# Two late stages of a twelve-layer network on one core: without TensorE's products of constants in its waits

## What is computed

```python
x = x + _L3_xattn_ref(_layernorm(x), ctx_1024, mask_BxS2_ik0, ...)   # stage 9
x = x + _L3_attn_ref(_layernorm(x), ...)                             # stage 10
x = x + _L3_ffn_ref(_layernorm(x), ...)                              # stage 11
```

## Time and profile before

| | |
|---|---|
| median of 3 runs | 1437.22 us (1436.2 to 1438.24) |
| profiled execution, its own time | 1435.54 us |
| span from first to last instruction | 1433.8 us |
| mean granted TensorE clock | 0.989 of full |
| busy share: PE, VectorE, ScalarE, GpSimd | 96%, 66%, 56%, 26% |
| stage 10, about | 1199.2 to 1253.5 us |
| stage 11, about | 1253.5 us to the end |

### The profile page before, as it was taken

The page is one execution under the profiler, slowest core; times in us unless marked ns, Lnnn a source line. Parts: engine busy times, 40 slices in busy tenths (PEclk is TensorE's granted clock), DMA queues, the critical chain, the costliest instruction groups (busy, mean ns, idle before and its releaser), DMA issues.

```text
span 1433.8 us, 24150 instructions
## 1 busy us (share of the span) xinstructions
PE 1376.1 (96%) x9532; PEld 973.4 (68%) x9541; DVE 953.4 (66%) x1559; ACT 805.6 (56%) x1481; POOL 370.4 (26%) x485
## 2 busy tenths in 40 slices
PE   7999999999999999999999989999999998999897
PEld 4897668886998676998567645555555554645686
DVE  5676744335786576786366578889999973566533
ACT  5774344344665555664555437778888884325232
POOL 3986332002642204542101332222121200100100
PEclk9999999999999999999999989999999999999999
DMA  9413342234214513212316255353535404210140
GB/s 372 156 56 132 129 171 81 89 95 166 97 60 152 194 60 126 97 60 76 130 72 272 76 198 167 121 183 123 194 129 183 152 2 189 89 59 2 59 177 15
DMA packets 49072, 177.77 MB, mean 124 GB/s; under 512 B 4864, under 2 KB 6144, under 8 KB 43008
## 3 DMA queue, kind: packets, MB, share of 16 engines
q1 hardware_dynamic: 48960, 176.23, 34.3%
HBM read 132.66 MB, written 44.60 MB: 124 GB/s over the span
## 4 chain that ended last, share of the span: by engine, by line
PE 74%; DVE 7%; ACT 3%; issue 1%; POOL 0%; ACTq 0%; DVEq 0%
PE PS L160 44%; PE PS L2387 9%; PE PS L2291 7%; PE PS L2305 4%; PE PS L630 2%; DVE SM L2402 2%; PE PS L1877 1%; PE PS L1898 1%; PE PS L2378 1%; PE PS L1905 1%; PE PS L2875 1%; PE PS L266 1%; DVE CNr L3094 0%; PE PS L1635 0%; ACT L283 0%
## 5 line engine op out<-in xcount | busy, mean ns | idle before, releaser
L2402 DVE TENSOR_REDUCE SM<-PS 128x1 f32<-128x1024 f32 x256 | 310.6, 1223 | 34.4 <-PE PS L2291 31.1
L160 PE MATMUL PS<-ARr 128*128 128x256 f32 (+1 forms) x1024 | 269.9, 335 | 0.5 <-POOL CNr L931 0.5
L160 PE MATMUL PS<-CNr,ARr 128*128 128x256 f32 (+1 forms) x952 | 199.1, 316 | 4.0 <-DVE ARr L792 3.7
L160 PEld LDWEIGHTS PS<-ARr 128*128 128x128 f32 x1024 | 179.9, 189 | 18.6 <-issue 0.8
L160 PEld LDWEIGHTS PS<-CNr,ARr 128*128 128x128 f32 x952 | 151.4, 190 | 18.6 <-DVE ARr L792 5.1
L160 PE MATMUL PS<-ARr,HTr 128*128 128x512 f32 x384 | 121.0, 396 | 0.5 <-ACT CN L459 0.5
L2291 PE MATMUL PS<-ARr 64*128 64x512 f32 x320 | 118.9, 454 | 0.7 <-DVE SM L2402 0.4
L2305 PE MATMUL PS<-ARr 64*128 64x256 f32 x640 | 116.5, 304 | 0.8 <-DVE ARr L2418 0.5
L853 ACT CAST ARr<-PS 128x512 fp32r<-128x512 f32 x96 | 56.2, 585 | 90.3 <-PE PS L630 90.1
L2470 ACT ACTIVATE AR<-PS 128x512 f32<-128x512 f32 x172 | 93.4, 605 | 16.8 <-PE PS L2305 13.4
L931 POOL TENSOR_TENSOR CNr<-CN,ARr 128x256 fp32r<-128x256 f32 x120 | 83.2, 728 | 72.0 <-ACT ARr L848 72.0
(11 more groups left out here) (412 smaller groups left out, 2756.0 us busy)
## 6 DMA issues: line engine op xcount, KB each, us to landing
CT<-k_tiles SPq DMA_DIRECT2D x64, 512.0 KB, 5.0
CN<-ctx_n SPq DMA_DIRECT2D x24, 1024.0 KB, 5.2
k_tiles<-CNr SPq DMA_DIRECT2D x32, 768.0 KB, 3.5
CT<-pack SPq DMA_DIRECT2D x6, 2048.0 KB, 8.1
v_ones<-CN SPq DMA_DIRECT2D x30, 288.0 KB, 2.8
CT<-ctx_t SPq DMA_DIRECT2D x8, 1024.0 KB, 19.1
k_tiles<-CN SPq DMA_DIRECT2D x32, 256.0 KB, 4.0
AR<-pack SPq DMA_DIRECT2D x16, 512.0 KB, 3.4
```

Of the source, the lines that this page charges most:

```text
L160: last = te.matmul(o, l, r, start=first and k == 0, stop=final and k == n - 1, skip_group_check=True)
L2402: ve.tensor_reduce(MX9[:, p % 2, e, g % 2, g % 8 // 2:g % 8 // 2 + 1], PS[:, b:b + 2, :].rearrange("p a b -> p (a b)"), AX, ALU.max).then_inc(
```

## The change

All nine calls of `keep_pe` in stages 10 and 11 go, with the products and the `take` calls in them. Nothing else is edited.

```diff
         def pe_10(pe):
             te = pe.e
-            keep_pe(pe, 13, 10, "norm")
             after(pe, 10)
             turn_all(pe, 10, "ht", H, "h")
...
                 z.then_inc(*pe.inc("mixed", "o_ps", 10, i))
-            keep_pe(pe, 7, 10, "out")
             wo = mat(W10["Wo"], 4)
...
         def pe_11(pe):
             te = pe.e
-            keep_pe(pe, 14, 11, "norm")
             after(pe, 11)
             turn_pe(pe, 11, "ht", H, "h", lambda i: [("ht", 11, i)])
-            keep_pe(pe, 9, 11, "turn")
...
                 if k:
                     row(k - 1)
-                if k > 4:
-                    keep_pe(pe, 5, 11, "best", k, ring=R11)
...
             pe_attend_11(pe, 1)
-            keep_pe(pe, 15, 11, "norm2")
             turn_all(pe, "11b", "ht", H, "h11")
-            keep_pe(pe, 3, 11, "turn2")
...
             z.then_inc(*pe.inc("proj", "lg_ps", 11))
-            keep_pe(pe, 10, 11, "choice")
...
                 if what == "dispatch":
-                    if e == 0:
-                        keep_pe(pe, 8, 11, "dispatch", e)
                     b, before = PB.take(("bt", e), ("bt", e))
```

## The result

The changed kernel takes 1444.44 us (median of 4 runs, 1443.14 to 1445.22), against 1436.71 us of the kernel before in the same call (4 runs). The medians differ by 7.7 us. The ratio is 1.0057, with a 95% interval from 1.0042 to 1.0072: 0.6% slower. The profiled execution took 1445.1 us, with a span of 1442.5 us; the mean granted clock went from 0.989 to 0.979.

What follows compares the result with a forecast made beforehand. TensorE, busy 96% of the span, was taken as the bound. Low-clock losses of 1.9 + 0.6 + 1.8 + 1.5 + 3.2 = 9.0 us on the 1437.22 median gave 1446.2 us, range 1441.0 to 1452.5 for eight in ten.

Steps and rivals of the forecast that it cites:

- the signs named: Clock 0.5 in parts of five places, 3 us idle before each norm's transposes, small products over 3 us, dispatch near 3.8.
- Start of stage 10: PE waits 3.4 us without constants, then transposes and dense products run at the low clock: 1.9 us, bounds 0.2 to 3.4.
- the 2.93 row: Trace row used as price: twelve products took 1.66 us at full clock, 2.93 at low; a low stretch loses 1.3 us.
- End of stage 10: PE waits 2.1 us, transposes, waits 0.77, then is dense; one chance in three of losing 1.7 us, taken as 0.6.
- Start of stage 11: Eight transposes in 7.0 us leave the clock low when the projections begin: 1.8 us, bounds 0.9 to 3.0.
- Units 5 to 7: Scores' maxima in stage 11: one chance in four that the clock falls, costing 6.0 us with the attention; taken as 1.5.
- Second norm to first expert: All runs at low clock: small products 1.4, dispatch 1.6, transposes 0.1, first expert 0.4, less 0.3 gained: 3.2 us.
- Banks: Removed `take` calls turn the PSUM bank order by one at each place; costed at nothing, a late bank up to 0.9 us.
- at either clock: Reading of the skill's weight-load formula: the router's sixteen small products would lose nothing, the sum being 1.4 us less.
- the low clock catches more: Rival, 17%: clock also falls at stage 10's end and units 5 to 7, lasting into the first expert: 14.8 us, 1452.
- The hidden fall: Rival, 6%: PE goes low in the waits but recovers with the first dense products; about 1 us lost, 1438.
- Late constants: Rival, 4%: groups of 13, 14 and 15 at low clock end over 2 us late; removing one such group gives 1435.2.

Runs made afterwards that it cites:

- stage 10 alone: The kernel before with only the 20 constants of stage 10 (13 and 7) gone: 1438.23 us against 1434.46, ratio 1.0024.
- takes only: The kernel before with all nine calls kept, banks taken and waited for, but 0 products in each: 1447.75 us, ratio 1.0081.
- the first four experiments: The kernel before without constants of stage 10, stage 11's start, units 5 to 7, or second norm to dispatch: ratios 1.0024, 1.0022, 1.0020, 1.0032.

## Why the prediction was right, and where it was off

The direction, the mechanism and the range (1441.0 to 1452.5) held: 1446.2 was forecast and 1444.44 measured, +9.0 and +7.7 us. That the two lie this close is partly luck: four executions in another call had a median of 1443.34 us, 9.3 above the kernel before there, and one of them, 1438.74, lies below the range. Of the signs named, the granted clock was low behind four of the places and not five, since the end of stage 10 kept it; the other signs came as said. By steps, from the distances of the changed kernel's profile:

- **Start of stage 10**: 1.9 forecast, 1.92 measured, in both pieces: 0.6 in the transposes, 1.3 in the first projections. The 1.3 is right for another reason than given. Only 2.6 us of the low stretch lay on the projections, and these lost half of it, where the forecast put a whole stretch of 3.4 us at the loss of the 2.93 row.
- **End of stage 10**: 0.6 forecast as one chance in three; 0 in two profiles of the changed kernel and 0.9 in two others (stage 10 alone, takes only). The price of 1.7 was too high; four profiles say little about the chance.
- **Start of stage 11**: 1.8 forecast, 1.7 and 1.6 measured, 2.3 and 3.0 in the two other runs, within the bounds 0.9 to 3.0. Here too the sum was right by other pieces than 1.3 and 0.5: the eight projections alone lost 1.65 us, half of the 3.3 us for which the clock was low under them, and what lay between them and unit 0 lost 0.1. For products of 512 columns the 2.93 row was too cheap a measure.
- **Units 5 to 7**: 1.5 forecast for units and attention together; 1.0 and 0 measured, 0 and 1.2 in the two profiles without their constants alone, 4.3 with takes only. The step had the place wrong: of the three profiles in which anything was lost here, two kept the units' period, and most of the loss was in the first attention steps in all three. Where the clock did fall in the units, a step went from 1.15 to 2.09 us, 0.9 and near the 1.1 per unit of the forecast, but for one step and not three.
- **Second norm to first expert**: 3.2 forecast, 3.0 measured. The small products cost 1.63 instead of 1.4, the dispatch 1.5 instead of 1.6, the transposes 0.34 instead of 0.1, the late constants gave back 0.45 instead of 0.3, and the first expert lost nothing (1.7 with takes only).
- **Banks**: costed at nothing, and takes only bears it out. That says nothing of rings whose banks others need at once: in stage 9 constants in a ring of three, with the wait and the low clock that followed, cost about 8 us by the ratio.

What separates 9.0 from 7.7 is in the two terms that were chances, 0.6 and 0.5 us too much; the base, the median shown, was 0.5 us higher than in the measuring call.

On the weight loads the row behind the earlier trace rows decides. The same sixteen products' loads, in the kernel before and in the changed one:

```profile
L160 PEld LDWEIGHTS PS<-AR,HT 128*128 128x128 f32 x15 | 1.8, 191 | 0.8 <-DVE HT L3043 0.8
```

```profile
L160 PEld LDWEIGHTS PS<-AR,HT 128*128 128x128 f32 x16 | 3.5, 330 | 1.4 <-issue 1.4
```

191 and 330 ns. The loads' mean grew 1.73 times and the sixteen products, 1.92 and 3.55 us, 1.85 times, so that the load's price goes with the granted clock here.

The Trainium skill ("TensorE: Matmul & The Clock Gate", LDWEIGHTS) gives a load as its columns over 1.2 and names no clock beside it; "at either clock" was the prediction's reading. So read, the formula would have put this place 1.6 us too low, and this trace does not agree with it.

Of the rivals, the one in which the low clock catches more was real: 14.8 us were worked out for it, and the execution with takes only lost 15.1 in stages 10 and 11. A changed kernel's execution of 1449.94 us with a clock of 0.975 points the same way, without a profile. It stood as another outcome of the change; it is more likely another execution of the same change. Which of its causes is right, sparse products or transposes that don't count, wasn't told apart, and no run varies them. The hidden fall was wrong: neither profile of the changed kernel lost less than 6.2 us. Late constants exist, at 0.45 us, but not at the groups of 13, 14 and 15: in every profile that has them they ran at full clock.

## What to carry to other kernels

Products of constants in a wait pay when the work behind the wait is TensorE's and on the path that sets the time, be it dense or, as at the router, small products behind their weight loads. They pay there, not in the wait: look for the granted clock in the first products behind each wait. Fit their number to the wait: at the start of stage 10 thirteen cost nothing, while none and twenty-six cost about the same. Give them a bank that nobody else needs, and compare distances between landmarks rather than medians when the effect is smaller than what one execution differs from the next.

## What the runs showed that was not expected

The spread between executions of one unchanged kernel goes mostly with the clock. In the 29 executions of the kernel before that ran beside the first four experiments, the nine with a mean clock of 0.994 or 0.995 took 1430.48 to 1432.11 us, and the ten with a clock of 0.987 to 0.990 took 1434.96 to 1438.13 us; the other ten lie between in clock, and all but one in time. The low level is met at other places in each: the profile of the kernel before has it at 498 and 666, that of the changed kernel at 349 and 455, in stages that the two have in common word for word.

In one call the changed kernel spread wider (four executions, 1438.74 to 1449.94 us) than the kernel before (eleven, 1431.93 to 1436.66); in the first call it did not (1443.14 to 1445.22 against 1435.65 to 1438.24). The constants may thus buy steadiness along with the 8 us, which two calls of four executions do not show.
